# A sparse-expert tail on one Trainium2 core: the first work list reversed, the last tile's rows in a place of their own, and the hand-over between the layers dealt anew

## The chip, the cores and the metric

One core of a Trainium2 chip runs the whole program. The metric is the device time of one execution in microseconds (us). TensorE (PE) multiplies and transposes, VectorE (DVE), ScalarE (ACT) and GpSimd (POOL) compute, SyncE (SP) only issues transfers; POOL issues the indirect ones. Each engine runs its own program in order and waits on semaphores.

## The reference, cut to what matters

```python
x = x + gnn(layernorm(x))                      # 3125 nodes, 256 wide, 50000 edges, two layers
logits = layernorm(x) @ router_w.T             # 8 experts
rw, re = top_k(softmax(logits), 2)             # each node picks two
for e in range(8):
    y = gelu(tokens @ w1[e] + b1[e]) @ w2[e] + b2[e]
    out = out + combine[:, e:e + 1] * y
```

## The kernel before, in words

The nodes lie in NT = 25 tiles of 128 rows; the last has 53. The first graph layer comes first. Then, until 446.33 us, a loop over the tiles t does the second and routes its rows: TensorE sums neighbours into PSUM; VectorE adds, takes the variance (`x2_and_var`), POOL the power (`root`), VectorE normalizes into a buffer `tok[t % KEPT]` (KEPT = 8) and stores the residual (`norm_and_sum`); TensorE turns the rows (`turn_token`) and scores them against the router (`score`). Every batch of 3 or 4 tiles is routed: `choose_experts` and `shares` (which needs ScalarE's Exp, `powers`), a prefix sum on TensorE (`prefix`), `place`, which gives each of a tile's two choices a row in a buffer `xs_dram` sorted by expert, and POOL's `scatter`, two indirect transfers for a tile.

A sorted expert's rows are worked in units of 256 rows (two halves of 128). For unit i SP loads the rows (`next_rows`), VectorE copies the expert's first weights (`keep_w1`) and the rows' node numbers and shares (`keep_meta`); TensorE transposes (`turn_rows`, L1635), multiplies into the hidden layer (`hidden`, L1644) and into the output (`result`, L1655); ScalarE copies the transposes (L1853), does the Gelu (L1859) and weighs the result (`weigh`, L1868); VectorE adds the bias (L1317); POOL adds each half into `out` by an indirect transfer that accumulates (`add_half`, L700 for the first 16 halves, L702 in the loop). I number the units from 0 and the halves from 0, so unit i has the halves 2i and 2i+1. The same node can stand in halves of two experts, so a half may have to wait until earlier halves have landed: `before_it`, read from the table `tab_wi`, says how many.

Experts are ranked by their counts in the first three batches. The first EARLY = 8 units are listed from the full units of the first four batches (`list_first`), so that they can begin while the last batch is still being routed. The rest of the list is made from all counts (`list_rest`) and starts again with rank 0. When the row counts are final (semaphore `ends`, in `place` of the last batch), SP writes 256 rows of padding behind each expert's last row (`pad_experts`, L431, eight transfers of 264 KB); unit 8's rows may be loaded only when all eight have landed (the wait at L575) and all scatters too.

The order of all this on each engine is written out by hand. Before the change VectorE runs, after the last tile: units 2 and 3 (weights, meta), `reached_by_batch` (L1263 to L1270), result 0, `choose_experts`, unit 4, result 1, `shares`, `place`, unit 5, result 2, `list_rest`, unit 6, result 3, `tables`, unit 7, result 4.

Of the kernel before, what the change touches and what calls it, by code (L numbers as in the profile page):

```python
# [5 lines left out]
F32 = mybir.dt.float32  # L6
# [3 lines left out]
ALU = mybir.AluOpType  # L10
# [4 lines left out]
P = 128  # L15
# [4 lines left out]
def build(nc, x, src, dst, w1l, w1r, b1, w2l, w2r, b2, router_w, ew1, eb1, ew2, eb2, out):  # L20
# [64 lines left out]
    with ExitStack() as ctx:  # L85
# [169 lines left out]
        at_row = later([1], F32)  # L255
        at_rest = later([1], F32)
# [32 lines left out]
        step_first = summed_first[:, NE - 3, :]  # L289
# [55 lines left out]
        rest = expert([NE], F32)  # L345
        tab_ef = expert([NTAB], F32)
# [89 lines left out]
        def _(sp):  # L436
# [160 lines left out]
        def _(pool):  # L597
# [59 lines left out]
            def scatter(t, j):  # L657

                pool.wait_ge(S["slots"], j + 1)
                pool.sem_inc(S["pool_held"], 1)  # L660
                for k in range(TOPK):
                    g.indirect_dma_start(xs_dram, bass.IndirectOffsetOnAxis(  # L662
                        ap=slots[:, t * TOPK + k:t * TOPK + k + 1], axis=0),
                        tok[t % KEPT], None).then_inc(scattered[t % 2], 16)
# [95 lines left out]
        def _(dve):  # L760
# [344 lines left out]
            def norm_and_sum(t):  # L1105

                k, alone = t % KEPT, t == 0
                dve.wait_ge(S["tok_free"], t + 1)
                dve.wait_ge(S["rstd_in"], t + 1)
                v.tensor_scalar(tok[k][:, 0:D], zt[:, :], stat[:, 6:7], stat[:, 8:9], ALU.subtract, ALU.mult  # L1110
                                ).then_inc(S["normed"], 1)
# [3 lines left out]
                v.tensor_tensor(uo, zt[:, :], tok[k][:, 0:D], ALU.add).then_inc(S["u_ready"], 1)  # L1115
# [49 lines left out]
            def place(j):  # L1165

                dve.wait_ge(S["prefix"], j + 1)
                of = prefix_of(j)
                link(v.tensor_tensor(pos, of[:, 0:BATCH * NE].rearrange("p (t e) -> p t e", e=NE),
                                     hist[:, j:j + 1, :].to_broadcast((P, BATCH, NE)), ALU.add))  # L1170
                last = v.tensor_tensor(hist[:, j + 1, :], hist[:, j, :], of[:, BATCH * NE:(BATCH + 1) * NE], ALU.add)
                if j == NB - 1:
                    link(last)
                    v.tensor_copy(end_i, hist[:, NB, :]).then_inc(S["ends"], 1)
                for k in range(TOPK):
                    last = v.tensor_tensor(posm.rearrange("p (t k) e -> p t k e", k=TOPK)[:, :, k, :],
                                           mask.rearrange("p (t k) e -> p t k e", k=TOPK)[:, :, k, :], pos, ALU.mult)
                link(last)
                for q in range(IN_BATCH[j]):
                    t = FIRST_OF[j] + q  # L1180
                    v.tensor_copy(tok[t % KEPT][:, D:XW], meta[:, t:t + 1, :].rearrange("p t c -> p (t c)"))
# [12 lines left out]
            def order_experts():  # L1194
# [15 lines left out]
                v.memset(id_step[:, NE - 1:NE], float(NE))  # L1210
                link(v.scalar_tensor_tensor(at_row, iota_e[:, 0:1], REGION / PAIR, at_p, ALU.mult, ALU.add))
# [11 lines left out]
            def list_first():  # L1223
# [5 lines left out]
                v.tensor_copy(first[:, 0:1], cum_first[:, 0:1])  # L1229
                link(v.tensor_tensor(first[:, 1:NE], cum_first[:, 1:NE], cum_first[:, 0:NE - 1], ALU.subtract))  # L1230
                v.tensor_scalar(first_h, first, 2.0, None, ALU.mult)
                v.tensor_scalar(skip_rest, id_step, REGION / PAIR, None, ALU.mult)
                link(v.scalar_tensor_tensor(step_first, id_step, REGION / PAIR, first, ALU.mult, ALU.subtract))
                v.scalar_tensor_tensor(at_rest, first[:, 0:1], float(-EARLY), at_row, ALU.add, ALU.add)
                v.tensor_tensor(skip_rest[:, 0:NE - 1], skip_rest[:, 0:NE - 1], first[:, 1:NE], ALU.add)
# [3 lines left out]
                v.scalar_tensor_tensor(bound_first, each_expert(cum_first[:, 0:NE - 1], n - 1), 2.0, got[:, 0:n - 1, 1:NE],  # L1239
                                       ALU.mult, ALU.add)  # L1240
                link(v.tensor_tensor(weight_first, up_first[:, 1:, 0:NE - 1], up_first[:, 0:n - 1, 0:NE - 1], ALU.subtract))
                v.tensor_scalar(entry_first[:, 0:1], entry_first[:, 0:1], at_row, 4.0, ALU.add, ALU.mult)
                v.tensor_scalar(entry_first[:, 1:2], entry_first[:, 1:2], iota_e[:, 0:1], None, ALU.add)
                link(v.scalar_tensor_tensor(terms_w, bound_first.rearrange("p b e -> p (b e)"), at_p,
# [8 lines left out]
            def tables(of, n, lo, hi, halves_too):  # L1253
# [4 lines left out]
                v.tensor_scalar(tab_wi[:, 2 * lo:2 * hi], of[:, 2 * n + 2 * lo:2 * n + 2 * hi], float(halves_too), None, ALU.add  # L1258
                                ).then_inc(S["table"], 1)

            def reached_by_batch():
# [8 lines left out]
                v.tensor_tensor(weight[:, 0:NB - 1, :], reached[:, NB + 1:, 0:NE - 1], reached[:, NB:2 * NB - 1, 0:NE - 1],  # L1270
                                ALU.subtract)
# [53 lines left out]
            def early_unit(i):  # L1325

                dve.wait_ge(S["hid"], i - 1)
                keep_w1(i, i % 2)
                keep_meta(i, i % 2, 16 * (i // 2 + 1))
# [4 lines left out]
            for t in range(NT):  # L1334
# [6 lines left out]
                if t == LIST_AT:  # L1341
                    dve.wait_ge(S["listed"], 1)
                    tables(bank[2], EARLY, 0, EARLY, 0)
# [28 lines left out]
            dve.wait_ge(S["listed"], 2)  # L1372
            tables(bank[0], NTAB, EARLY, NTAB, 2 * EARLY)
# [14 lines left out]
        def _(pe):  # L1388
# [178 lines left out]
            def turn_token(t):  # L1567
                pe.wait_ge(S["normed"], t + 1 + NT)
                pe.wait_ge(S["nrm_t_in"], t + 2 * NT)
                for c in range(KD):  # L1570
                    last = te.transpose(bank[0][:, c * P:(c + 1) * P], tok[t % KEPT][:, c * P:(c + 1) * P], ident[:, :])  # L1571
                last.then_inc(S["nrm_tr"], 1)
# [75 lines left out]
            def result(i, s):  # L1648
                e = pe.value_load(tab_ei[0:1, bass.ds(i, 1)], min_val=0, max_val=NE - 1)
# [22 lines left out]
            def early_round(i):  # L1672

                result(i, i % 2)
# [7 lines left out]
            for i in range(4):  # L1682
                early_round(i)
            list_units(spread, bank[0], 2)
            for i in range(4, EARLY):
                early_round(i)
# [10 lines left out]
        def _(act):  # L1697
# [223 lines left out]
```

## Time and profile before

| | |
|---|---|
| median of 3 runs | 585.8 us (585.45 to 586.36) |
| the profiled execution, its own time | 586.81 us |
| its span in the trace | 584.8 us |
| busy: PE, DVE, ACT, POOL | 94%, 63%, 39%, 32% |
| granted TensorE clock, mean | 0.99 |

The span is that of one profiled execution and lies 2.0 us under its own time and 1.0 us under the median. Times in the trace are us from the start of the span.

### The profile page before, as it was taken

The numbers are of one execution on the slowest core, as the hardware profiler recorded it, in microseconds if no ns is written. First come the engines' busy times: TensorE is split into PE (matmuls) and PEld (weight loads), VectorE is DVE, ScalarE is ACT, GpSimd is POOL, SyncE is SP. The second block draws the span as 40 slices with busy tenths as digits, with TensorE's granted clock in tenths as the row PEclk, the third lists the DMA queues.
The fourth block names the chain that finished last, engine by engine and source line by source line (L and its number), as shares of the span: only waits on it lengthen the run. The fifth ranks groups of instructions, "written<-read, shape, count | busy, mean of one in ns | idle before, by whom it ended". The sixth has DMA issues, their size and how long they took to land.

```text
span 584.8 us, 11275 instructions
## 1 busy us (share of the span) xinstructions
PE 551.6 (94%) x3023; PEld 332.0 (57%) x3024; DVE 367.7 (63%) x1256; ACT 225.2 (39%) x427; POOL 185.1 (32%) x180
## 2 busy tenths in 40 slices
PE   5899999999999999999999999999998878999992
PEld 3445555555555555555445555555555767888881
DVE  6898677667676766765345667667877753444441
ACT  4666944444443444543100100000004544555652
POOL 4661000000000000000031034443446687587886
PEclk9999999999999999999999999999999989999997
DMA  8431121011011110111562135764335498668774
GB/s 255 143 91 55 55 63 55 29 55 54 28 55 42 41 55 28 55 49 33 119 208 82 55 118 181 239 214 137 127 102 179 120 253 139 122 127 130 124 127 47
DMA packets 64347, 61.29 MB, mean 105 GB/s; under 512 B 11281, under 2 KB 62334, under 8 KB 64302
## 3 DMA queue, kind: packets, MB, share of 16 engines
q1 hardware_dynamic: 48510, 45.92, 26.0%
q0 software_dynamic: 11200, 14.40, 13.0%
q10 hardware_dynamic: 4592, 0.41, 0.6%
q8 instruction: 23, 0.38, 0.3%
q14 instruction: 22, 0.18, 0.1%
HBM read 32.34 MB, written 29.30 MB: 105 GB/s over the span
## 4 chain that ended last, share of the span: by engine, by line
PE 71%; issue 9%; DMA 8%; DVE 5%; POOL 3%; POOLq 2%; ACT 0%; DVEq 0%; SPq 0%; ACTq 0%
PE bank L1497 22%; PE counts_ps L1497 13%; PE bank L1412 8%; PE bank L1487 7%; PE counts_ps L746 7%; PE bank L1655 5%; PE counts_ps L1644 5%; DMA out<-adj 3%; POOL xs_dram L662 2%; DMA y<-y_dram 2%; PE counts_ps L1635 1%; POOLq L690 1%; DMA xs_dram<-w,onehots 1%; PE bank L1402 1%; PE bank L1480 1%
## 5 line engine op out<-in xcount | busy, mean ns | idle before, releaser
L1497 PE MATMUL bank<-y,adj 128*128 128x512 f16 x625 | 154.7, 379 | 0.4 <-ACT zt L1731 0.4
L1497 PE MATMUL counts_ps<-y,adj 128*128 128x512 f16 x625 | 144.2, 379 | 1.9 <-DMA y<-y_dram 1.9
L753 ACT ACTIVATE adj<-counts_ps 128x1000 f32 (+1 forms) x80 | 80.2, 1004 | 59.0 <-PE counts_ps L746 59.0
L1497 PEld LDWEIGHTS counts_ps<-y,adj 128*128 128x128 f16 x625 | 60.5, 101 | 64.5 <-DMA y<-y_dram 4.2
L1497 PEld LDWEIGHTS bank<-y,adj 128*128 128x128 f16 x625 | 57.9, 97 | 59.5 <-issue 13.7
L639 POOL IOTA onehots<- 128x8 int32 x1 | 0.1, 143 | 225.7 <-PE counts_ps L746 225.7
L702 POOL DMA_INDIRECT out<-adj x40 | 62.9, 1572 | 18.2 <-issue 8.8
L1644 PE MATMUL counts_ps<-adj 128*128 128x256 f32 x240 | 56.9, 381 | 0.4 <-ACT adj L1853 0.4
L1655 PE MATMUL bank<-adj 128*128 x224 | 54.9, 389 | 2.4 <-issue 2.4
L746 PEld LDWEIGHTS counts_ps<-onehots 125*128 125x128 f16 x640 | 42.5, 98 | 23.9 <-ACT adj L753 11.2
L732 DVE TENSOR_TENSOR onehots<-iota,lo_t 125x1024 f16<-125x1024 f16 x80 | 54.9, 686 | 1.7 <-issue 0.9
L732 DVE TENSOR_TENSOR onehots<-iota,key_t 125x1000 f16<-125x1000 f16 x80 | 53.8, 673 | 0.0
L1830 ACT ACTIVATE rows<-bank 128x256 f32<-128x256 f32 x25 | 9.6, 382 | 113.3 <-PE bank L1571 113.3
L746 PE MATMUL counts_ps<-onehots 125*128 125x125 f16 x640 | 51.0, 221 | 0.5 <-DVE onehots L732 0.5
L1412 PE MATMUL bank<-w,rows 128*128 128x512 f32 x100 | 48.2, 604 | 3.0 <-issue 1.6
L1644 PEld LDWEIGHTS counts_ps<-adj 128*128 128x128 f32 x240 | 45.2, 190 | 7.1 <-ACT adj L1848 0.6
L1487 PE MATMUL bank<-w,rows 128*128 128x512 f32 x100 | 47.0, 592 | 0.0
L1655 PEld LDWEIGHTS bank<-adj 128*128 128x128 f32 x224 | 41.4, 195 | 8.0 <-issue 3.3
L1868 ACT ACTIVATE adj<-adj 128x256 f32<-128x256 f32 x56 | 25.4, 503 | 41.2 <-DVE adj L1317 41.2
L655 POOL TENSOR_TENSOR stat<-stat 128x1 f32<-128x1 f32 x25 | 14.2, 567 | 73.8 <-DVE stat L1103 73.8
L1724 ACT ACTIVATE yo<-bank,scl_i 128x256 f16<-128x256 f32 x23 | 10.9, 473 | 58.7 <-PE bank L1487 58.7
L1317 DVE TENSOR_TENSOR adj<-bank,adj 128x512 f32<-128x512 f32 x28 | 19.4, 692 | 20.7 <-PE bank L1655 18.8
(283 smaller groups left out, 670.9 us busy)
## 6 DMA issues: line engine op xcount, KB each, us to landing
adj<-xs_dram SPq DMA_DIRECT2D x31, 264.0 KB, 3.2
rows<-z_dram SPq DMA_DIRECT2D x49, 128.0 KB
z_dram<-zt SPq DMA_DIRECT2D x33, 128.0 KB, 1.7
adj<-in_L_ffn_w SPq DMA_DIRECT2D x16, 256.0 KB, 3.2
rows<-in_x SPq DMA_DIRECT2D x24, 128.0 KB
out<-yo SPq DMA_DIRECT2D x24, 128.0 KB
y_dram<-yo SPq DMA_DIRECT2D x23, 128.0 KB, 1.7
y<-y_dram SPq DMA_DIRECT2D x4, 640.0 KB, 6.8
```

Of the source, the lines that this page charges most:

```text
L655: g.tensor_tensor(stat[:, 8:9], stat[:, 9:10], stat[:, 10:11], ALU.pow).then_inc(S["rstd_in"], 1)
L702: g.indirect_dma_start(out, at, ye[u][:, h, :], None, bounds_check=N - 1, oob_is_err=False, compute_op=ALU.add).then_inc(landed[q % NLAND] ...
L732: last = nc.vector.tensor_tensor(oh[0:RUN, slot, :].rearrange("p (g k w) -> p g k w", k=n, w=HALF), iota_4[0:RUN, 0:n, :].rearrange("p (g ...
L746: last = nc.tensor.matmul(counts_ps[:, 2 * slot + bank_of, at * P:at * P + KEYS], stat_g[:, :, h:h + 1].rearrange("p k a -> p (k a)"), mov ...
L753: nc.scalar.activation(adj[:, :, bass.ds(at, GW * WD)].rearrange("p b (h d) -> p b h d", d=WD), counts_ps[:, 2 * (group % 2):2 * (group % ...
L1317: v.tensor_tensor(ysum[s], y_ps[s], ew(eb2_sb, e, 0).rearrange("p (h n) -> p h n", h=1) .to_broadcast((P, 2, D)), ALU.add).then_inc(S["ysu ...
L1412: last = te.matmul(out_of[t % 2][:, :], nrm_t_of[t % 2][:, k * P:(k + 1) * P], w[:, k, :], start=(k == 0), stop=(k == KD - 1))
L1487: last = te.matmul(bank[1][:, :], nrm_t[:, k * P:(k + 1) * P], w[:, k, :], start=(k == 0), stop=(k == KD - 1))
L1497: last = te.matmul(to, adj[:, b, t * P:(t + 1) * P], y[:, b, :], start=(b == 0), stop=(b == NT - 1))
L1644: last = te.matmul(hid_ps[s][:, m * PAIR:(m + 1) * PAIR], w1_of[s][:, k, m * P:(m + 1) * P], xe_t[s][:, k * PAIR:(k + 1) * PAIR], start=(k ...
L1655: last = te.matmul(y_ps[s][:, h, :], ge_t[s][:, m * PAIR + h * P:m * PAIR + (h + 1) * P], ew(ew2_sb, e, m), start=(m == 0), stop=(m == KD ...
L1868: a.activation(ye[u][:, h, :], ysum[s][:, h, :], ACT.Copy, scale=tab_c[:, bass.ds(i * 2 + h, 1)]).then_inc(S["ye_in"], 1)
```

## The change

- **First list reversed.** The first 8 units come in the reverse order of the ranks, so that the last of them and unit 8 are of the same expert (rank 0). `list_first` finds a position p by `at_rev` = 7 - p and `at_less` = p - 16 instead of `at_p`; the number added to `before_it` in the rest of the list is no longer 16 but 16 less the halves of rank 0 in the first list (`list_base`), and those are added back for every later expert (one more instruction in `reached_by_batch`).
- **Own place for the last tile's rows.** Tile 24 is normalized into `tok_last` and no longer into the buffer of tile 16. POOL therefore doesn't wait, after the scatter of tile 17, until that of tile 16 has landed.
- **The tail's order.** On VectorE result 0 comes straight after unit 3; `shares` follows `choose_experts`; unit 4 is split, its weights before result 1 and its meta after `place`; `reached_by_batch` comes after result 2, and `list_rest` after unit 6. ScalarE does the last Exp before the transposes of unit 3 and the Gelu of unit 2, and the dummy Gelu is gone. SP loads unit 6 before it writes the first three paddings, and writes five after unit 7 where it wrote two. TensorE reads the expert number of a unit (`expert_of`) one unit ahead in the first 8 units, and multiplies out the rest of the list (`list_units`) after result 4 and not before it.

```diff
@@ SP
-            row = row_of(6)
+            next_rows(6, row_of(6))
+            row = row_of(7)
             pad_experts(sp, range(0, 3))
-            next_rows(6, row)
-            row = row_of(7)
-            pad_experts(sp, range(3, 6))
             next_rows(7, row)
-            pad_experts(sp, range(6, NE))
+            pad_experts(sp, range(3, NE))
@@ POOL, scatter
-                if 0 < t <= NT - KEPT:
+                if 0 < t < NT - KEPT:
                     pool.wait_ge(scattered[(t - 1) % 2], ((t - 1) // 2 + 1) * (16 * TOPK))
                     pool.sem_inc(S["tok_free"], 1)
@@ DVE, list_first
-                v.scalar_tensor_tensor(terms_2, cum_first, at_p, id_step, ALU.is_le, ALU.mult, accum_out=entry_first[:, 1:2])
-                v.scalar_tensor_tensor(terms_1, cum_first, at_p, step_first, ALU.is_le, ALU.mult, accum_out=entry_first[:, 0:1])
+                v.scalar_tensor_tensor(terms_2, cum_first, at_rev, id_step, ALU.is_le, ALU.mult, accum_out=entry_first[:, 1:2])
+                v.scalar_tensor_tensor(terms_1, cum_first, at_rev, skip_rest, ALU.is_le, ALU.mult, accum_out=entry_first[:, 0:1])
+                v.tensor_scalar(list_base, first_h[:, 0:1], -1.0, float(2 * EARLY), ALU.mult, ALU.add)
@@ DVE, reached_by_batch
+                v.tensor_tensor(weight[:, 0, 0:1], weight[:, 0, 0:1], first_h[:, 0:1], ALU.add)
@@ DVE, after the last tile
             early_unit(2)
             early_unit(3)
-            reached_by_batch()
             early_result(0)
             choose_experts(NB - 1)
-            early_unit(4)
+            shares(NB - 1)
+            early_weights(4)
             early_result(1)
-            shares(NB - 1)
             place(NB - 1)
+            early_meta(4)
             early_unit(5)
             early_result(2)
+            reached_by_batch()
+            early_unit(6)
             list_rest()
-            early_unit(6)
             early_result(3)
             dve.wait_ge(S["listed"], 2)
-            tables(bank[0], NTAB, EARLY, NTAB, 2 * EARLY)
+            tables(bank[0], NTAB, EARLY, NTAB, list_base)
@@ PE
+            e = expert_of(0)
+            for i in range(EARLY):
+                result_of(e, i, i % 2)
+                if i + 1 < EARLY:
+                    e = expert_of(i + 1)
...
+                if i == 4:
+                    list_units(spread, bank[0], 2)
                 hidden(i + 2, i % 2)
                 turn_rows((i + 3) % 2, 16 * ((i + 3) // 2 + 1))
@@ ACT
                 if i == 0:
                     weigh(0, 0, 0)
+                    powers(NB - 1)
+                    turn_rows(3, 1)
                 gelu(i + 2, i % 2)
-                turn_rows(i + 3, (i + 3) % 2)
-                if i == 0:
-                    powers(NB - 1)
-                    a.activation(scl[:, 14:15], scl[:, 8:9], ACT.Gelu)
-                else:
+                if i > 0:
+                    turn_rows(i + 3, (i + 3) % 2)
                     weigh(i, i // UNITS, i % UNITS)
```

On VectorE, between unit 3's meta (L1302) and result 0 (L1314, L1317), the program before holds the seven instructions of `reached_by_batch`:

```order
L1302 SCALAR_TENSOR_TENSOR adj<-adj 128x2 x2
L1263 TENSOR_TENSOR adj<-onehots 128x56
L1265 TENSOR_SCALAR adj<-adj 128x56
L1266 TENSOR_SCALAR adj<-adj 128x112
L1267 CAST adj<-adj 128x112
L1268 TENSOR_TENSOR adj<-adj,onehots 128x112
L1269 TENSOR_SCALAR adj<-adj 128x112
L1270 TENSOR_TENSOR adj<-adj 128x42
L1309 TENSOR_LOAD adj
L1309 ISA x2
L1314 CAST adj<-adj 128x2
L1317 ISA
```

The changed program has at the same place on VectorE (its line numbers are some 8 higher; L1134 is the first instruction of `choose_experts`):

```order
L1310 SCALAR_TENSOR_TENSOR adj<-adj 128x2 x2
L1317 TENSOR_LOAD adj
L1317 ISA x2
L1322 CAST adj<-adj 128x2
L1325 ISA
L1325 TENSOR_TENSOR adj<-bank,adj 128x512
L1134 COPY onehots<-bank 128x32
```

So result 0 stands directly behind unit 3 there, and the seven are now behind result 2.

On SP, after the load of unit 5, the program before reads unit 6's row number (L522) and goes straight to the first padding (L430, L431), which waits for `ends`:

```order
L525 DMA adj<-xs_dram 128x2x264
L522 TENSOR_LOAD adj
L522 ISA x2
L430 TENSOR_LOAD onehots [waits zeros,ends]
L430 ISA x2
L431 ISA
L431 DMA xs_dram<-biases 128x2x264
```

The changed program issues unit 6's load (L532) first, which waits for `meta_in` and `xe_tr`, and only then the first padding (L437, L438):

```order
L529 TENSOR_LOAD adj
L529 ISA x2
L532 ISA [waits meta_in,xe_tr]
L532 DMA adj<-xs_dram 128x2x264
L529 TENSOR_LOAD adj
L529 ISA x2
L437 TENSOR_LOAD onehots [waits zeros,ends]
L437 ISA x2
L438 ISA
L438 DMA xs_dram<-biases 128x2x264
```

The load of unit 6 has moved from behind three paddings to ahead of all eight, and with it the paddings are now queued behind unit 4's meta.

On ScalarE, behind the weighing of unit 0 (L1888), the changed program has the Exp (L1854), unit 3's transposes (L1873) and then unit 2's Gelu (L1879), each function with its table load:

```order
L1888 ACTIVATE adj<-adj 128x256 [waits landed1]
L1854 ACT_TABLE_LOAD
L1854 ACTIVATE onehots<-onehots 128x32 [waits top]
L1873 ACTIVATE adj<-counts_ps 128x512 [waits xe_tr]
L1876 TENSOR_LOAD adj
L1876 ISA x2
L1879 ISA [waits hid]
L1879 ACT_TABLE_LOAD
```

Before, the Gelu and the transposes stood ahead of the Exp; the number of table loads is the same.

## Rows read from the trace of the kernel before

**Rows 1.** The page: the span
```profile
span 584.8 us, 11275 instructions
```

**Rows 2.** The chain in order of time: start, us, what; pieces of the tail
```profile
478.65 4.41 DMA out<-adj
483.26 3.34 DMA adj<-xs_dram
...
576.03 3.68 DMA out<-adj
...
580.78 1.55 POOL out L702
```

**Rows 3.** POOL's timeline: halves 10, 15, 16, 54; in brackets the idle time before
```profile
489.79 1.55 POOL L700 DMA_INDIRECT out<-adj  x1 [2.18 <-ACT adj L1868]
...
499.69 1.55 POOL L700 DMA_INDIRECT out<-adj  x1 [0.31 <-DMA out<-adj]
505.62 1.55 POOL L702 DMA_INDIRECT out<-adj  x1 [4.39 <-issue]
...
577.88 1.55 POOL L702 DMA_INDIRECT out<-adj  x1 [0.31 <-issue]
```

**Rows 4.** ScalarE's timeline: a table load; units 5, 8 and 27 weighed
```profile
461.31 1.28 ACT L1834 ACT_TABLE_LOAD   x1
...
488.48 0.91 ACT L1868 ACTIVATE adj<-adj 128x256 f32<-128x256 f32 x2 [0.54 <-DVE adj L1317]
...
498.49 0.91 ACT L1868 ACTIVATE adj<-adj 128x256 f32<-128x256 f32 x2 [1.07 <-DVE adj L1317]
...
572.57 0.91 ACT L1868 ACTIVATE adj<-adj 128x256 f32<-128x256 f32 x2 [1.41 <-DVE adj L1317]
```

**Rows 5.** TensorE's timeline: last tile, result 4, hidden 7, transposes 8, result 6
```profile
453.12 0.44 PE L1571 MATMUL bank<-ident,w 128*128 128x128 f32 x2 [1.05 <-DVE w L1110]
...
474.87 3.54 PE L1655 MATMUL bank<-adj 128*128 x8 [1.24 <-issue]
...
483.46 1.89 PE L1644 MATMUL counts_ps<-adj 128*128 128x256 f32 x8
486.65 0.66 PE L1635 MATMUL counts_ps<-ident,adj 128*128 128x128 f32 x4 [1.30 <-DMA adj<-xs_dram]
487.56 1.99 PE L1655 MATMUL bank<-adj 128*128 x8 [0.25 <-issue]
```

**Rows 6.** SP's queue in time: the last two paddings
```profile
477.25 1.50 SPq L431 DMA_DIRECT2D xs_dram<-biases  x2
```

**Rows 7.** SP's instructions of L575, 477.3 to 480: duration in ns, first and last start
```profile
L575 SPq EVENT_SEMAPHORE  x1: 3375/3375/3375, 479.5 to 479.5; - x1
```

**Rows 8.** POOL's timeline: the first scatter of tile 18
```profile
446.96 1.20 POOL L662 DMA_INDIRECT xs_dram<-w,onehots  x1 [2.74 <-DMA xs_dram<-w,onehots]
```

**Rows 9.** VectorE's timeline: last norm, reached, result 0, choose's end, ends, slots
```profile
452.65 0.41 DVE L1110 TENSOR_SCALAR w<-zt,stat 128x256 f32<-128x256 f32 x1 [1.99 <-POOL stat L655]
...
455.63 0.21 DVE L1263 TENSOR_TENSOR adj<-onehots 128x56 int32<-128x56 f32 x1
...
457.30 0.20 DVE L1270 TENSOR_TENSOR adj<-adj 128x42 f32<-128x42 f32 x1
...
458.45 0.69 DVE L1317 TENSOR_TENSOR adj<-bank,adj 128x512 f32<-128x512 f32 x1
...
461.75 0.16 DVE L1152 TENSOR_TENSOR onehots<-onehots 128x16 f16<-128x16 f16 x1
...
465.78 0.17 DVE L1174 CAST onehots<-onehots 128x8 int32<-128x8 f32 x1
...
466.83 0.17 DVE L1187 CAST onehots<-onehots 128x8 uint32<-128x8 f32 x1
```

**Rows 10.** Windows: us, PE busy, PEld, DVE, ACT, POOL, granted clock, DMA share, GB/s
```profile
472.00:474.00 2.00, 0.72 (x5) 0.52 (x5) 1.76 (x12) 1.20 (x3) 1.70 (x2) 1.00 0.80 298
...
476.00:477.00 1.00, 1.00 (x4) 0.82 (x3) 0.68 (x4) 0.79 (x2) 0.69 (x2) 0.50 1.06 267
```

More of the change, by code:

```diff
@@ L255, in build @@
         at_row = later([1], F32)
+        at_rev = later([1], F32)
+        at_less = later([1], F32)
+        list_base = later([1], F32)
         at_rest = later([1], F32)
@@ L345, in build, with tok_of @@
         rest = expert([NE], F32)
+        tok_last = expert([XW], F32)
+        def tok_of(t):
+            return tok[t % KEPT] if t < NT - 1 else tok_last
         tab_ef = expert([NTAB], F32)
@@ L1105, in norm_and_sum @@
             def norm_and_sum(t):
-                k, alone = t % KEPT, t == 0
-                dve.wait_ge(S["tok_free"], t + 1)
+                alone = t == 0
+                dve.wait_ge(S["tok_free"], min(t + 1, NT - 1))
                 dve.wait_ge(S["rstd_in"], t + 1)
-                v.tensor_scalar(tok[k][:, 0:D], zt[:, :], stat[:, 6:7], stat[:, 8:9], ALU.subtract, ALU.mult
+                v.tensor_scalar(tok_of(t)[:, 0:D], zt[:, :], stat[:, 6:7], stat[:, 8:9], ALU.subtract, ALU.mult
                                 ).then_inc(S["normed"], 1)
@@ L1180, in place @@
                     t = FIRST_OF[j] + q
-                    v.tensor_copy(tok[t % KEPT][:, D:XW], meta[:, t:t + 1, :].rearrange("p t c -> p (t c)"))
+                    v.tensor_copy(tok_of(t)[:, D:XW], meta[:, t:t + 1, :].rearrange("p t c -> p (t c)"))
                 link(v.tensor_reduce(slot_f, posm, AX.X, ALU.add))
@@ L1210, in order_experts @@
                 v.memset(id_step[:, NE - 1:NE], float(NE))
+                v.tensor_scalar(at_rev, at_p, -1.0, float(EARLY - 1), ALU.mult, ALU.add)
+                v.tensor_scalar(at_less, at_p, float(-2 * EARLY), None, ALU.add)
                 link(v.scalar_tensor_tensor(at_row, iota_e[:, 0:1], REGION / PAIR, at_p, ALU.mult, ALU.add))
@@ L1229, in list_first @@
                 v.tensor_copy(first[:, 0:1], cum_first[:, 0:1])
+                v.tensor_scalar(skip_rest, id_step, REGION / PAIR, None, ALU.mult)
                 link(v.tensor_tensor(first[:, 1:NE], cum_first[:, 1:NE], cum_first[:, 0:NE - 1], ALU.subtract))
                 v.tensor_scalar(first_h, first, 2.0, None, ALU.mult)
-                v.tensor_scalar(skip_rest, id_step, REGION / PAIR, None, ALU.mult)
-                link(v.scalar_tensor_tensor(step_first, id_step, REGION / PAIR, first, ALU.mult, ALU.subtract))
@@ L1234, in list_first @@
                 v.scalar_tensor_tensor(at_rest, first[:, 0:1], float(-EARLY), at_row, ALU.add, ALU.add)
-                v.tensor_tensor(skip_rest[:, 0:NE - 1], skip_rest[:, 0:NE - 1], first[:, 1:NE], ALU.add)
-                v.scalar_tensor_tensor(terms_2, cum_first, at_p, id_step, ALU.is_le, ALU.mult, accum_out=entry_first[:, 1:2])
-                v.scalar_tensor_tensor(terms_1, cum_first, at_p, step_first, ALU.is_le, ALU.mult, accum_out=entry_first[:, 0:1])
+                link(v.tensor_tensor(skip_rest[:, 0:NE - 1], skip_rest[:, 0:NE - 1], first[:, 1:NE], ALU.add))
@@ L1251, in list_first, with tables @@
                 last.then_inc(S["spread"], 1)
-            def tables(of, n, lo, hi, halves_too):
+            def tables(of, n, lo, hi, base):
                 v.tensor_scalar(tab_ri[:, lo:hi], of[:, lo:hi], float(PAIR // 4), float(NE * REGION), ALU.mult, ALU.min)
@@ L1325, in early_unit, with early_weights, early_meta @@
             def early_unit(i):
+                early_weights(i)
+                early_meta(i)
+            def early_weights(i):
                 dve.wait_ge(S["hid"], i - 1)
                 keep_w1(i, i % 2)
+            def early_meta(i):
                 keep_meta(i, i % 2, 16 * (i // 2 + 1))
@@ L1342, in _ @@
                     dve.wait_ge(S["listed"], 1)
-                    tables(bank[2], EARLY, 0, EARLY, 0)
+                    tables(bank[2], EARLY, 0, EARLY, 0.0)
                 norm_and_sum(t)
@@ L1570, in turn_token @@
                 for c in range(KD):
-                    last = te.transpose(bank[0][:, c * P:(c + 1) * P], tok[t % KEPT][:, c * P:(c + 1) * P], ident[:, :])
+                    last = te.transpose(bank[0][:, c * P:(c + 1) * P], tok_of(t)[:, c * P:(c + 1) * P], ident[:, :])
                 last.then_inc(S["nrm_tr"], 1)
@@ L1648, in result, with result_of @@
             def result(i, s):
-                e = pe.value_load(tab_ei[0:1, bass.ds(i, 1)], min_val=0, max_val=NE - 1)
+                result_of(pe.value_load(tab_ei[0:1, bass.ds(i, 1)], min_val=0, max_val=NE - 1), i, s)
+            def result_of(e, i, s):
                 pe.wait_ge(S["ge_in"], i + 1)
@@ L1670, in _, with expert_of @@
             pe.sem_inc(S["ysum_in"], 2)
-            def early_round(i):
-                result(i, i % 2)
+            def expert_of(i):
+                return pe.value_load(tab_ei[0:1, bass.ds(i, 1)], min_val=0, max_val=NE - 1)
+            e = expert_of(0)
[3 more added lines that the diff above has]
+                    e = expert_of(i + 1)
                 if i == 0:
@@ L1678, in early_round @@
                     prefix(NB - 1)
+                if i == 4:
+                    list_units(spread, bank[0], 2)
                 hidden(i + 2, i % 2)
                 turn_rows((i + 3) % 2, 16 * ((i + 3) // 2 + 1))
[L1682 to L1686, printed above, removed]
             pe.wait_ge(S["table"], 2)
```

19 lines of the change are left out of this document (9 added, 10 removed).

## The prediction

> **What bounds the kernel now.** Everything the change touches lies in the last quarter of the span [rows 1], so I started at the end of the chain of waits and read back. The last unit's second half (half 55) starts on POOL at 580.78, 1.07 us after the transfer of half 53, begun at 576.03, has landed (3.68 later, 579.71) [rows 2]. Before that POOL issues one half after another. From half 16 at 505.62 to half 54 at 577.88 are 38 steps in 72.26 us, 1.90 each [rows 3]. ScalarE has weighed what POOL issues long before: unit 8 is weighed from 498.49, its first half starts at 505.62, 7.13 later; for unit 27 it is 572.57 and 577.88, 5.31 later [rows 3, 4]. Where POOL really waits for ScalarE, the step is 1.31 (unit 5: 488.48 to 489.79 [rows 3, 4]). So from 505.62 on POOL sets the end, though the chain names TensorE for most of that stretch: it follows the semaphore that came last by its record. The date of half 16 is what has to be explained.
>
> Half 16 follows half 15 (499.69) by 5.93 us, an idle time of 4.39 that the trace calls issue [rows 3]. No engine's work ends it. But in the program before every half of the rest of the list asks for at least 16 landed halves, so half 16 needs the landing of half 15, issued just before it.
>
> Half 15 in turn hangs on unit 7, and that on TensorE's stream, which last stood still before unit 8's transposes at 486.65, waiting for that unit's rows [rows 5]. They were loaded at 483.26, and here the chain puts the wait down to a transfer of POOL's from 478.65 [rows 2], which is again only the last record. SP's own instructions show it: the wait at L575, for the eight paddings, lasts 3.375 us from 479.5 to 482.9 [rows 7]. The last padding was issued by 477.25 + 1.50 = 478.75 [rows 6] and so landed 4.1 later. SP had started on the paddings as soon as `ends` was set, at 465.78 + 0.17 = 465.95 on VectorE [rows 9], and worked through them and two loads without waiting for anybody.
>
> **The change, step by step.**
>
> *The last norm.* POOL idled 2.74 us before tile 18's scatter for the landing of tile 16's [rows 8]; VectorE then idled 1.99 for POOL's power and TensorE 1.05 for VectorE's norm [rows 5, 9]. With a place of its own for tile 24 the first is gone. POOL's power comes 2.35 earlier at most (two scatters are still ahead of it, and VectorE's variance), so VectorE gains its 1.99 and TensorE its 1.05.
>
> *Result 0.* `reached_by_batch` takes 455.63 to 457.50, 1.87 us, and no longer stands ahead of it. Result 0 goes from 458.45 to 458.45 - 1.99 - 1.87 = 454.6. TensorE's side: last turn at 453.12 - 1.05 = 452.1, 0.44 for it, some 2.1 for the result, 454.6 too.
>
> *From result 0 to `ends`.* Now 465.95 - 458.45 = 7.5 us, with choose, unit 4, result 1, shares and half of `place` in it [rows 9]. The same pieces are there afterwards in another order, but unit 4's meta (0.4) has gone behind `place`, whose rest takes 467.0 - 465.95 = 1.05. So meta 4 ends at 454.6 + 7.5 + 1.05 = 463.15. `shares` now waits early for the Exp: ScalarE weighs unit 0 from 455.3 for 0.91, loads the table in 1.28 [rows 4] and is done near 457.8; choose ends 461.91 - 458.45 = 3.46 after result 0 [rows 9], at 458.1. It fits with 0.3 to spare. Unit 2's Gelu, behind both table loads, ends near 460.5, half a us before TensorE wants it; should it be late, TensorE has slack (below). The Trainium skill (ScalarE: Activation LUTs, Table sets) puts a switch of tables at about 2.7 us. The trace has 1.28, and by that figure the Exp, hence everything to the end, would come 1.1 us later than I say.
>
> *SP.* Unit 6's load and all paddings now wait for meta 4 (463.15) where they waited for `ends` (465.95). Behind that SP does the same eight paddings, two loads and two reads of row numbers as before, only in another order. So the last padding is issued 2.8 us earlier, near 476.0, and unit 8's rows are loaded at 480.5 instead of 483.26, if the landing still takes 4.1. The bounds: 0, if the transfers themselves are the limit; and at most as much as TensorE could use, next.
>
> *TensorE.* It reads the expert number ahead, which saves the 0.25 before result 6 [rows 5]. After `list_units` (VectorE: meta 4 at 463.15, then unit 5, result 2, the seven moved instructions, unit 6 and `list_rest`, together 9.7 us, so 472.9 as now) it has hidden 6, transposes 7, result 5 and hidden 7 left, 5.9 us: done at 479. Now hidden 7 ends at 483.46 + 1.89 = 485.35. So without the rows of unit 8 being late TensorE would gain 6; with them at 480.5 + 3.34 = 483.85 it gains 2.8 + 0.25 = 3.05 and stands idle for nearly 5 us, where it now stands for 1.30.
>
> *The clock.* That idle time has a price. Between 471.7 and 474.87 TensorE did almost nothing (0.72 busy in 472 to 474), and then ran at 0.50 of its clock, 1.2 GHz and not 2.4 [rows 10]: result 4 took 3.54 us, against 1.99 for result 6, 1.55 lost [rows 5]. Now this loss is hidden, because it falls ahead of the wait for unit 8. Afterwards the long pause comes last, and the slow stretch lies on result 6 and hidden 8, in the open. I charge 1.55 once. Left for TensorE: 1.5. Bounds 3.05 (no fall) and about 0 (a longer slow stretch).
>
> *Half 16.* The added number becomes 16 less the halves of rank 0 in the first list. Counting the router's choices for the reference's inputs, ranks 0, 1, 2 get 3, 3, 2 of the 8 units; so half 16 asks for 10, all long landed. What is left of the 5.93 is between one plain step, 1.90, and one issue plus the 1.07 that POOL needs from the end of a wait to its next transfer, 1.55 + 1.07 = 2.62 [rows 2, 3]. Nothing says that its loop is entered without cost, so I take 2.62: 3.3 us saved, 4.0 at most. Within the first list, reversed, halves 4 and 5 ask for the halves three places back instead of five and six, 5.6 us back at 1.86 a step, more than the landings of 3.7 to 4.4 [rows 2]. No new wait.
>
> *Other edits.* The few added instructions of `order_experts` and `list_first` lie under TensorE's sums of a tile; uncovered they would be some 0.2 us each. POOL reaches half 2 some 4 us earlier, since `slots` does (467.0 to 462.7 [rows 9]); halves 2 to 15 then fill 26 us and aren't the limit at a gain under 6.
>
> *Sum.* Half 15 starts 1.5 earlier, half 16 1.5 + 3.3 = 4.8. Does POOL still set the end? Its lag behind ScalarE at unit 8 falls from 7.13 to 3.8, and by the 1.8 that it makes up over the loop to 2.0 at unit 27, over the 1.31 of a real wait. It does, barely. So the span goes from 584.8 to 580.0, and the median, 1.0 above the span [rows 1], from 585.8 to **581.0**.
>
> **The rivals.**
> - *No fall of the clock.* TensorE's pause is split by other work, as now at 485.35, where 1.3 idle left the clock alone. Then 3.05 + 3.3 = 6.35: 579.5. Against it: the pause I expect is longer than the one before 474.87.
> - *The paddings land no sooner.* The DMA share is 0.80 at 472 to 474 and 1.06 at 476 to 477 [rows 10]; if bytes and not issues are the limit, unit 8's rows come when they do now, and only 0.25 + 3.3 less the clock's 1.55 is left, 2.0: 583.8. The Trainium skill (DMA: Bandwidth & Descriptors, Issuing engines are not separate DMA queues) says that transfers of all issuing engines interleave on the same 16 engines; POOL's adds begin earlier here and so run into the paddings. For the gain speaks that before 470 these engines were half idle, and the paddings move there.
> - *Unit 8's rows are not late.* If the padding goes out much faster ahead of POOL's adds, TensorE gets near its 6: 6 + 3.3 gives 576.7 at best.
> - *The list change doesn't do it.* If the 4.39 at half 16 is the entry into POOL's loop and no landing, 1.5 remains: 584.3. Against it: ScalarE enters its own loop with 1.07 idle [rows 4].
> - *Slower.* One mechanism could do it, the clock. At 0.50 each us costs half a us. If TensorE, once slow after a pause of 5 us, stayed so, the 6.35 would be eaten after 12.7 us of it, and each unit more would cost 3.9 us. Up to now one slow stretch ended by itself before result 5.
>
> **How the numbers follow.** Chances: as forecast 0.45, no fall of the clock 0.24, paddings no sooner 0.12, unit 8 not late 0.06, list change without effect 0.07, slower 0.03, the rest spread. A measurement here tells 0.2% (1.2 us) from no change. Faster by more: all but about half of the list case, and the slower one: 0.88; within 0.2%: 0.09; slower: 0.03. The range takes in the forecast with its bounds (clock, 4.0 for half 16) and the first two rivals: 577.6 to 584.3.
>
> **What would show it.** VectorE's last norm without its 1.99 idle; result 0 near 454.6; slots at 462.7; SP's wait for the paddings still there, ending near 480.1; TensorE idle for 4 us or more before unit 8's transposes near 483.9; a stretch at 0.50 right behind it; and half 16 at most 2.7 us after half 15, near 501. I would be wrong if the gap of half 16 stayed above 4, if the paddings took over 5 us to land, or if POOL in the loop showed waits for ScalarE.

## The result and the profile after

The changed kernel takes 582.55 us (median of 5 runs, 580.24 to 583.07) against 586.24 for the kernel before beside it: ratio 0.9933, interval 0.9915 to 0.9952. Two more sets on other chips, `after_again` and `after_third`, gave 0.9930 each. (One execution of the kernel before, beside `after_again`, took 1163.3 us and is left out of the ratios.) The forecast of 581.0 had the sign, and its range the time; it was 1.55 too low. Of these, 0.44 is the kernel before itself, which took 586.24 beside it and not 585.8: the gain was 3.7 where 4.8 was forecast.

The profiled execution took 583.07 with a span of 581.2, where [rows 1] has 584.8, and where the tail begins it runs 0.44 earlier than that of before. That much is chance: the traces of `after_again` and `after_third` reach this place 1.3 and 1.4 later than this one. TensorE's timeline (start, us, in brackets the idle time before), lines 1652 transposes, 1674 results, 1661 hidden layers:

```profile
451.48 0.38 PE L1588 MATMUL bank<-ident,adj 128*128 128x128 f32 x2
...
476.33 1.89 PE L1661 MATMUL counts_ps<-adj 128*128 128x256 f32 x8
482.92 1.12 PE L1652 MATMUL counts_ps<-ident,adj 128*128 128x128 f32 x4 [4.70 <-DMA adj<-xs_dram]
483.83 3.62 PE L1674 MATMUL bank<-adj 128*128 x8
487.24 1.98 PE L1661 MATMUL counts_ps<-adj 128*128 128x256 f32 x8
489.06 0.60 PE L1652 MATMUL counts_ps<-ident,adj 128*128 128x128 f32 x4
```

The rows of [rows 5] are all there, earlier, but the pause before unit 8's transposes has grown from 1.30 to 4.70 and result 6 takes 3.62 instead of 1.99. The windows (stretch, its length, busy time of PE, PEld, DVE, ACT and POOL, then the granted clock, the DMA share and GB/s) show the clock falling behind the pause:

```profile
477.00:480.00 3.00, 1.22 (x6) 0.74 (x4) 0.00 (x0) 1.10 (x3) 2.39 (x3) 1.00 0.95 163
480.00:484.00 4.00, 1.08 (x5) 1.08 (x6) 0.63 (x7) 0.00 (x0) 2.35 (x2) 0.57 0.97 198
484.00:487.00 3.00, 3.00 (x9) 2.37 (x8) 1.61 (x8) 1.51 (x3) 0.98 (x1) 0.50 0.60 130
```

SP's queue; the last of the four paddings is issued by 470.81 + 4.87 = 475.68, and unit 8's rows are asked for at 479.22:

```profile
470.81 4.87 SPq L438 DMA_DIRECT2D xs_dram<-biases  x4
479.22 1.76 SPq L532 DMA_DIRECT2D adj<-xs_dram  x2
```

Between them stands SP's instruction of L580, the wait for the eight paddings (ns, least, median, most; the long one is 2,512 from 476.3 on, so to 478.8, where [rows 7] has 3,375):

```profile
L580 SPq EVENT_SEMAPHORE  x2: 28/1270/2512, 476.3 to 478.9; - x2
```

VectorE: last norm, result 0, `ends`, `slots`. The 1.99 of idle time of [rows 9] is gone:

```profile
450.00 0.41 DVE L1115 TENSOR_SCALAR adj<-zt,stat 128x256 f32<-128x256 f32 x1
...
453.82 0.69 DVE L1325 TENSOR_TENSOR adj<-bank,adj 128x512 f32<-128x512 f32 x1 [0.24 <-PE bank L1674]
...
460.72 0.17 DVE L1179 CAST onehots<-onehots 128x8 int32<-128x8 f32 x1
...
461.87 0.19 DVE L1192 CAST onehots<-onehots 128x8 uint32<-128x8 f32 x1
```

ScalarE: units 3, 8 and 27 are weighed. Ahead of unit 3 it stands idle for 4.41:

```profile
473.47 0.91 ACT L1888 ACTIVATE adj<-adj 128x256 f32<-128x256 f32 x2 [4.41 <-DVE adj L1325]
...
496.43 0.91 ACT L1888 ACTIVATE adj<-adj 128x256 f32<-128x256 f32 x2 [1.06 <-DMA out<-adj]
...
570.68 0.91 ACT L1888 ACTIVATE adj<-adj 128x256 f32<-128x256 f32 x2 [1.60 <-DVE adj L1325]
```

POOL: a scatter that no longer waits, then halves 15, 16, 17, 38, 39, 54, 55:

```profile
444.10 0.96 POOL L667 DMA_INDIRECT xs_dram<-w,onehots  x1 [0.30 <-issue]
...
497.63 1.55 POOL L705 DMA_INDIRECT out<-adj  x1 [0.30 <-DMA out<-adj]
500.18 1.55 POOL L707 DMA_INDIRECT out<-adj  x1 [1.00 <-DMA out<-adj]
502.30 1.55 POOL L707 DMA_INDIRECT out<-adj  x1 [0.57 <-DMA out<-adj]
...
543.43 1.73 POOL L707 DMA_INDIRECT out<-adj  x1 [0.31 <-issue]
545.47 1.55 POOL L707 DMA_INDIRECT out<-adj  x1 [0.30 <-issue]
...
574.21 1.55 POOL L707 DMA_INDIRECT out<-adj  x1 [0.30 <-issue]
577.14 1.55 POOL L707 DMA_INDIRECT out<-adj  x1 [1.38 <-issue]
```

Against [rows 3], half 15 starts 2.06 earlier and half 16 5.44 earlier. But half 54 starts only 3.67 earlier. Between them lie 74.03 us for 38 steps, where before there were 72.26: 1.77 of the gain is given back inside the loop. POOL's lag behind ScalarE (start of a unit's first half less start of its weighing) goes from 3.75 at unit 8 to 3.53 at unit 27, where I had it fall to 2.0. This is what the experiments had to explain first.

One row above gives a hint: half 38's transfer is 1.73 long, not 1.55. From unit 8 on 12 transfers of the even halves last over 1.6 us, up to 1.79, and the start after a long one comes later. VectorE at that place:

```profile
542.46 0.69 DVE L1325 TENSOR_TENSOR adj<-bank,adj 128x512 f32<-128x512 f32 x1 [0.76 <-PE bank L1674]
543.32 0.43 DVE L1330 COPY adj<-adj 128x512 f32 x1 [0.17 <-issue]
```

The copy of the weights starts at 543.32, 0.11 ahead of POOL's 543.43. At each of the long ones it starts 0.05 to 0.19 ahead, and in the kernel before at five of its six (units 15 and 20 to 23, at a lag near 6; the sixth is in unit 11, where the copy starts 1.14 behind POOL). A unit takes POOL 3.71 where it is free, and the copies come every 3.89 as TensorE does. So my theory was: POOL gains on ScalarE until its start falls just behind a copy's, and then each unit's gain is taken back; one such lag is near 6.0, another near 4.0, and the changed kernel starts its loop at 3.75.

### The profile page after: what moved, and what is told of

Same layout as the page of the kernel before. It is cut to its first block, busy times and chain, and to the rows that moved or that the text cites. A ratio compares the mean times of both kernels' runs of the same rounds, so it can differ in the third digit from the quotient of the medians.

```text
span 581.2 us, 11275 instructions
## 1 busy us (share of the span) xinstructions
PE 551.5 (95%) x3023; PEld 332.8 (57%) x3024; DVE 366.5 (63%) x1259; ACT 225.1 (39%) x426; POOL 184.7 (32%) x180
## 4 chain that ended last, share of the span: by engine, by line
PE 64%; issue 11%; DMA 11%; POOL 5%; DVE 4%; POOLq 4%; ACT 0%; SPq 0%; DVEq 0%; ACTq 0%
PE bank L1514 23%; PE counts_ps L1514 13%; DMA out<-adj 8%; PE bank L1429 8%; PE counts_ps L751 7%; PE bank L1504 7%; POOLq L695 2%; POOL xs_dram L667 2%; DMA y<-y_dram 2%; PE bank L1419 1%; POOLq L700 1%; PE bank L1674 1%; PE bank L1497 1%; POOL out L707 1%; PE bank L1599 1%
## 5 line engine op out<-in xcount | busy, mean ns | idle before, releaser
L707 POOL DMA_INDIRECT out<-adj x40 | 64.2, 1604 | 15.3 <-issue 7.5
L1429 PE MATMUL bank<-w,rows 128*128 128x512 f32 x100 | 49.4, 617 | 2.1 <-issue 2.0
L1504 PE MATMUL bank<-w,rows 128*128 128x512 f32 x100 | 47.0, 592 | 0.0
L1888 ACT ACTIVATE adj<-adj 128x256 f32<-128x256 f32 x56 | 25.4, 503 | 38.8 <-DVE adj L1325 32.3
```

Of the source, the lines that this page charges most:

```text
L707: g.indirect_dma_start(out, at, ye[u][:, h, :], None, bounds_check=N - 1, oob_is_err=False, compute_op=ALU.add).then_inc(landed[q % NLAND] ...
L1429: last = te.matmul(out_of[t % 2][:, :], nrm_t_of[t % 2][:, k * P:(k + 1) * P], w[:, k, :], start=(k == 0), stop=(k == KD - 1))
L1504: last = te.matmul(bank[1][:, :], nrm_t[:, k * P:(k + 1) * P], w[:, k, :], start=(k == 0), stop=(k == KD - 1))
L1888: a.activation(ye[u][:, h, :], ysum[s][:, h, :], ACT.Copy, scale=tab_c[:, bass.ds(i * 2 + h, 1)]).then_inc(S["ye_in"], 1)
```

## The experiments

**The list alone** (`list_alone`). The kernel before with the edits of the change that belong to the list, and nothing else (cut):

```diff
-                v.scalar_tensor_tensor(terms_2, cum_first, at_p, id_step, ALU.is_le, ALU.mult, accum_out=entry_first[:, 1:2])
+                v.scalar_tensor_tensor(terms_2, cum_first, at_rev, id_step, ALU.is_le, ALU.mult, accum_out=entry_first[:, 1:2])
...
-            tables(bank[0], NTAB, EARLY, NTAB, 2 * EARLY)
+            tables(bank[0], NTAB, EARLY, NTAB, list_base)
```

> The kernel before with the reversed first list and nothing else of the change. If the 5.93 us between halves 15 and 16 were the wait for a landing, the gap becomes 2.6 and half 16 starts 3.3 earlier, near 502.3. If the pause is the entry into POOL's loop, the gap stays 5.9 and the time stays 585.8. What reaches the end depends on the second theory, the one on POOL's slow transfers: POOL's lag behind ScalarE would be 3.8 at unit 8, and if a copy on VectorE holds POOL at a lag of about 4 it is still about 3.5 at unit 27 (before 5.3): 1.8 us gained, 584.0. If nothing holds it there, POOL goes on at 1.86 a half until it waits for ScalarE at a lag of 1.3 to 2: all 3.3 gained, 582.5.

Ratio 0.9974 (0.9953 to 0.9995): 1.5 us faster. POOL at half 16:

```profile
497.15 1.55 POOL L703 DMA_INDIRECT out<-adj  x1 [0.30 <-DMA out<-adj]
500.04 1.66 POOL L705 DMA_INDIRECT out<-adj  x1 [1.34 <-DMA out<-adj]
```

The gap is 2.89. The lag at unit 8 is 4.09, 13 transfers are long, and it is still 3.48 at unit 27. The wait for a landing is shown, and so is that less than the 3.3 reaches the end: the interval allows 2.7 at most. Beside it, TensorE's pauses of 1.93 and 0.98 brought no fall of the clock (1.00 from 478 to 490).

**The change without its list** (`list_undone`), the same edits taken out of the changed kernel.

> The changed kernel with the first list in rising order of ranks again. Landing theory: the gap before half 16 goes from 2.55 back to 5.9, half 16 near 503.5, lag behind ScalarE 7.1 at unit 8. With the hold at a lag of 4 in the changed kernel, this one catches up as the kernel before did, to 5.3 at unit 27, and loses only about 1.8: 584.4. Without such a hold it loses 3.3: 585.9. If the list does nothing: 582.5.

Ratio 0.9983 (0.9966 to 1.0000); half 16 5.73 after half 15, lag 6.93 and then 5.88. Since the changed kernel hadn't run on this chip, I ran it again beside it (`list_undone_2`):

> The first list in rising order of ranks again, beside the changed kernel. Half 16 comes 5.7 us after half 15 and not 2.6, which puts POOL's lag behind ScalarE at 7 instead of 4 at unit 8. At a lag of 7 no copy of VectorE meets POOL's transfers, so this kernel catches up by about 1 to 1.2 us over the loop and the changed one by none: 2.0 us slower than the changed kernel (range 1.2 to 3.1). Rival, no hold: 3.1 slower.

583.90 (0.9979, 0.9961 to 0.9997) against 581.31 for the changed kernel (`after_third`): the list is worth 2.6, between the two theories. By the spread of the two sets it can be 0.9 more or less, so this doesn't tell 2.0 from 3.1. Half 16 with its old wait:

```profile
501.12 1.55 POOL L708 DMA_INDIRECT out<-adj  x1 [3.94 <-issue]
```

**Tile 24 in tile 16's place** (`tok_undone`).

```diff
-            return tok[t % KEPT] if t < NT - 1 else tok_last
+            return tok[t % KEPT]
...
-                if 0 < t < NT - KEPT:
+                if 0 < t <= NT - KEPT:
...
-                dve.wait_ge(S["tok_free"], min(t + 1, NT - 1))
+                dve.wait_ge(S["tok_free"], t + 1)
```

> The changed kernel with tile 24's rows again in the place of tile 16's. Theory that this wait was on the path: POOL waits 2.7 us before tile 18's scatter again, VectorE's last norm comes some 2 us later (452.3 for 450.0), result 0 at 455.8, and with it slots, paddings and unit 8's rows; unit 8's transposes 2 us later and the end too: 584.5. Rival: Exp, tables and paddings have enough slack of their own, so result 0 moves and unit 8's rows do not: within 0.5 of 582.5.

The median was 583.62 (0.9980, 0.9958 to 1.0001), yet in the profiled execution unit 8's transposes came no later than in the changed kernel. The two didn't agree, so again beside the changed kernel (`tok_undone_2`):

> Tile 24's rows in the place of tile 16's again, now beside the changed kernel. In the first run's trace result 0 came 1.75 us later (455.57 for the weighing of unit 0, half 2 at 469.05 for 468.05), yet unit 8's transposes came as in the changed kernel, since the landing of the paddings takes up the difference. Theory from that: no difference on the path, within 1 us of the changed kernel. Rival, from the first run's median (0.9980 of before, where the changed kernel has 0.993): about 2.5 us slower than the changed kernel.

582.97 (0.9967, 0.9948 to 0.9987) against 581.31: 1.7 slower. The two sets together, each against the kernel before beside it, put this kernel 2.4 behind the changed one (by my estimate from their spread 1.4 to 3.3), so my theory of no difference is wrong. POOL in this execution:

```profile
446.40 0.96 POOL L667 DMA_INDIRECT xs_dram<-w,onehots  x1 [2.26 <-DMA xs_dram<-w,onehots]
```

And TensorE, unit 8's transposes:

```profile
485.28 1.11 PE L1652 MATMUL counts_ps<-ident,adj 128*128 128x128 f32 x4 [4.78 <-DMA adj<-xs_dram]
```

The wait is back, unit 0 is weighed at 456.82 instead of 455.92 in the changed kernel beside it, and unit 8's transposes start at 485.28 instead of 483.68. A single pair of traces can't price the wait: in the three traces of the changed kernel itself unit 0 is weighed at 454.54, 455.80 and 455.92, and the last padding lands 2.9 to 3.9 behind its issue in the traces of these kernels.

**The copy in another mode** (`reduce_copy`; the edit is cut, and holds from unit 8 on).

```diff
-                v.tensor_copy(w1_of[s].rearrange("p k n -> p (k n)"),
-                              ew1_sb[:, bass.ds(e, 1), :].rearrange("p a n -> p (a n)")).then_inc(S["w1_in"], 1)
...
+                    last = v.tensor_reduce(to, of.rearrange("p (n b) -> p n b", b=1), AX.X, ALU.add)
```

> The changed kernel, where VectorE moves the weights of units 8 to 27 with a sum over an axis of one element instead of the copy: the same bytes, another mode of the engine (about 0.6 to 0.7 us instead of 0.43). Theory: POOL's transfers take 1.66 to 1.79 us instead of 1.55 in the even halves of units 9 to 14 and 18 to 24 because the fast copy starts with them and keeps POOL out. Then all of them take 1.55, POOL's step falls from 3.89 to 3.71 a unit, its lag behind ScalarE falls from 3.5 to between 1.3 and 2 at unit 27, and the time to 580.5 to 581.0. The Trainium skill (SBUF - State Buffer, Who interferes with whom) says that a copy in the two-port mode and a GpSimd instruction shut each other out and that tensor_reduce never contends. Rival: the longer transfers are POOL's own or the DMA engines' (the same halves stay long), time 582.5; or the longer VectorE instruction delays TensorE and it is slower.

POOL's transfers from half 16 on (ns, least, median, most), first in the changed kernel, then here:

```profile
L707 POOL DMA_INDIRECT out<-adj x40: 1547/1549/1794, 500.2 to 577.1; - x40
```

```profile
L707 POOL DMA_INDIRECT out<-adj x40: 1547/1549/1566, 500.3 to 576.2; - x40
```

Not one is long, although VectorE's instruction now lasts 0.69. It isn't that the two no longer meet: here too some begin 0.10 to 0.19 behind VectorE's instruction, as half 42:

```profile
551.20 0.69 DVE L1334 TENSOR_REDUCE adj<-adj 128x512 f32 x1 [0.16 <-issue]
551.30 1.55 POOL L707 DMA_INDIRECT out<-adj  x1 [0.30 <-issue]
```

So it is the form of the copy, not its bytes and not the timing. By the Trainium skill (SBUF — State Buffer, Who interferes with whom) a copy in a two-port mode and an instruction of GpSimd exclude each other, and whichever begins first shuts the other out for the whole of its length. The trace agrees that the copy holds up the transfer and the reduction doesn't, but not on the rest. The price is at most 0.24 of the copy's 0.43, and a copy that begins at 568.70 in the kernel before, 0.09 behind a transfer of POOL's, takes its 0.43. What the 40 transfers take over 1.55 each sums to 2.2 us in the changed kernel's first trace, and to nothing here. The time, however, was 581.69 (0.9941, 0.9920 to 0.9961), no better than the changed kernel's ratio, and the lag at unit 27 was 2.81, not under 2. Two things stand behind that. POOL has other short waits here, 0.55 to 0.65 before halves 24 to 27, put down to landings; and the hold is not always there: in the three traces of the changed kernel 12, 8 and 3 transfers are long, and in the third the lag does fall, from 3.77 to 2.16 in 72.36 us. From half 16 to 54 the 2.2 us of the long transfers are gone in `reduce_copy`, but POOL's other waits have grown by 1.4, and these steps take 73.27 us, only 0.76 less than 74.03. So it is shown that the copy lengthens the transfers; that this alone costs the end of the kernel anything is not. In `list_undone` only one transfer is long, and the lag still falls by no more than 1.05.

**Three paddings on ScalarE** (`split_pads`), and the changed kernel beside it (`after_again`, 581.50).

```diff
-            pad_experts(sp, range(3, NE))
+            pad_experts(sp, range(3, SP_PADS))
...
+                    if i == 3:
+                        pad_experts(act, range(SP_PADS, NE))
                     weigh(i, i // UNITS, i % UNITS)
```

(`SP_PADS` is 5.)

> The changed kernel, where ScalarE issues the last three of the eight paddings ahead of the third unit's weighing, at about 469 to 473, where it stands idle for 4.41 us. Theory: what holds unit 8's rows is SP's issuing (last padding at 475.3) and a landing of some 3 us behind it. Then SP has issued its last near 471 and ScalarE near 473, the wait ends near 476, unit 8's rows are asked for near 476.5 instead of 479.2 and TensorE's transposes start near 480 instead of 482.9, with a pause under 2 us and no fall of the clock (result 6 in 2.0 instead of 3.6): 2.9 + 1.6, so about 4 us less than the changed kernel beside it. Rival: the bytes on the DMA engines are the limit (paddings and adds together), the wait ends when it does now, near 478.8, and the time is the changed kernel's.

577.84 (0.9877, 0.9854 to 0.9901), 3.7 less than the changed kernel (1.5 to 5.2 by the spread of the two sets). ScalarE's issues lie in its idle time:

```profile
468.49 3.57 ACTq L440 DMA_DIRECT2D xs_dram<-biases  x3
473.17 0.91 ACT L1890 ACTIVATE adj<-adj 128x256 f32<-128x256 f32 x2 [5.09 <-DVE adj L1327]
```

TensorE waits 0.68 for unit 8's rows, where the changed kernel waits 4.70 in its first trace and 2.38 in that of `after_again`, and result 6 takes 1.89:

```profile
479.68 0.67 PE L1654 MATMUL counts_ps<-ident,adj 128*128 128x128 f32 x4 [0.68 <-DMA adj<-xs_dram]
480.18 1.89 PE L1676 MATMUL bank<-adj 128*128 x8
```

In `after_again` the two were:

```profile
483.54 0.66 PE L1652 MATMUL counts_ps<-ident,adj 128*128 128x128 f32 x4 [2.38 <-DMA adj<-xs_dram]
484.04 3.22 PE L1674 MATMUL bank<-adj 128*128 x8
```

SP's wait for the paddings ends at 476.1 instead of 478.8 in the changed kernel's first trace, so the rival, that bytes set the time, is out. The same edit in the kernel before (`before_split`):

> The kernel before, where ScalarE issues the last three paddings ahead of unit 3's weighing and nothing else is changed. Theory: paddings are worth only what TensorE can use, and here it has its own work until 485.35 and waits 1.30 us for unit 8's rows; half 16 waits for the landing of half 15 as before. So at most 1.3 us faster, and perhaps nothing, since ScalarE weighs unit 3 up to 1.5 us later: 0.997 to 1.001 of the kernel before. Rival: the paddings are the bound on their own, whatever the order of the rest, and it gains the 3 to 4 us that they gave in the changed kernel.

0.9990 (0.9972 to 1.0008): nothing that stands out of the noise, and 1.6 us at most. There SP's wait ended at 481.2 (before 482.9) and half 16 waited as ever, so the paddings are worth their 3.7 only behind the rest of the change.

**Filling TensorE's pause** (`filled`).

```diff
                 hidden(i + 2, i % 2)
+                if i == 5:
+                    for _ in range(38):
+                        te.transpose(bank[1][:, 0:P], ident[:, :], ident[:, :])
                 turn_rows((i + 3) % 2, 16 * ((i + 3) // 2 + 1))
```

> The changed kernel with 38 idle transposes (128x128, 0.11 us each, about 4.1 us) on TensorE behind hidden 7, which nobody reads. Theory: the pause of 4.7 us before unit 8's transposes drops the clock to 0.50, and result 6 costs 3.6 instead of 2.0. With the filling the clock stays at 1.0, result 6 takes 2.0, results 6 and 7 come 1.6 earlier and the end 1.6 earlier than that of the changed kernel beside it. Rival: the slow stretch has its cause further ahead (the 2.5 us without work before list_units at 472), the clock falls all the same and the time is the changed kernel's, or up to 0.5 more if the filling reaches past the rows' arrival.

579.36 (0.9894, 0.9879 to 0.9908), 2.1 less than the changed kernel (0.2 to 3.4 by the spread of the two sets). TensorE's timeline, L1708 being the filling:

```profile
480.51 4.31 PE L1708 MATMUL bank<-ident 128*128 128x128 f32 x38
484.66 0.60 PE L1652 MATMUL counts_ps<-ident,adj 128*128 128x128 f32 x4
485.09 1.89 PE L1674 MATMUL bank<-adj 128*128 x8
```

From 478 to 490 the clock stays at 1.00 and result 6 takes 1.89, although TensorE does nothing useful in these 4.31 us. The rival is out: here too the clock fell further ahead (0.57 from 474 to 476, after the 2.49 without work before `list_units`), and it had come back before result 6. The filling reaches about 1 us past the rows' arrival, so that unit 27 is weighed only 0.6 earlier than in `after_again`'s trace. The rest of that pair's difference is POOL's lag at unit 27 (2.28 for 4.02), which the filling doesn't touch. So it is shown that the filling holds the clock; of the 2.1, the traces put no more than 0.6 down to it.

**Both** (`split_reduce`).

> Both: three paddings on ScalarE, and VectorE's move of the weights from unit 8 on as a sum over one element. If both theories hold the time is the changed kernel's less 4 (paddings) and less 0.7 (the reduced hold, as far as the run alone showed: lag 2.8 instead of 3.5 at unit 27). If POOL becomes the bound once TensorE is 4.5 earlier, the second part is worth more, up to 2 us, since POOL then runs at 1.85 a half without the steps of 2.05.

575.91 (0.9835, 0.9812 to 0.9859): 9.6 us faster than before, and the best kernel here. Over `split_pads` it gains 1.9, more than the copy's mode gave alone, but by the spread of the two sets it can be anything from nothing to 3.8. Its lag fell only from 3.97 to 3.07, against 3.92 to 3.21 in `split_pads`, so it isn't shown that this gain comes from the hold.

The tail's new order was never undone by itself. Undoing the list costs 2.6 and undoing tile 24's own place costs 1.7. Together that is already more than the 3.7 of the change, so the parts don't simply add up, and what the order is worth stays open.

## Why the prediction was right, and where it failed

- **Last norm, result 0.** Predicted 454.6, measured 453.82, or 454.26 with the 0.44 of this execution; in the other two traces of the changed kernel unit 0 is weighed 1.3 later than here. The wait is gone; it is worth 1.7 at the end (`tok_undone_2`).
- **From result 0 to `slots`.** Predicted 462.7, measured 461.87 + 0.19. The Exp came in time, with tables loaded in 1.28 each.
- **SP.** The last padding was issued at 475.7 (predicted 476.0). The landing term was mis-sized: 3.1 behind it and not 4.1, so unit 8's rows were asked for at 479.22 and not 480.5. That the transfers themselves are not the limit, `split_pads` shows.
- **TensorE and its clock.** A pause of nearly 5 was predicted, 4.70 came, and the slow stretch behind it. Charged were 1.55; result 6 alone lost 1.63, the transposes 0.5 more. This and the earlier rows about cancel, which is luck: half 15 starts 2.06, 1.94 and 2.08 earlier in the three traces, against 1.5 in the sum. `filled` shows that with work in the pause result 6 isn't slow.
- **Half 16.** Predicted 2.62 behind half 15, measured 2.55, and 2.57 in the other two traces. Shown both ways, by `list_alone` and `list_undone_2`.
- **The step that failed** is in the sum: "by the 1.8 that it makes up over the loop to 2.0 at unit 27". I took the rate of catching up from the kernel before, as if it belonged to POOL alone. In the profiled execution it made up 0.2: from half 16 to 54 it needed 74.03 us and not 72.26. Of these 1.77 us, 1.31 are longer transfers, which come from where POOL's starts lie against VectorE's copies, and 0.46 short waits. Half 16 had come 5.44 earlier where the sum has 4.8, so the last halves come 1.1 later than in the sum, as the gain of 3.7 falls short of 4.8 by 1.1. In the other two traces of the changed kernel POOL lost 0.3 (that execution took 583.32) and made up 1.6 (581.38). What sets the rate as a whole stays open, since without any long transfer it was 0.96 in `reduce_copy`.
- **Rivals.** Paddings that land no sooner, a list without effect, rows that aren't late and a clock that stays up: none occurred. Two side sums were off. TensorE's gain without late rows was counted from the end of hidden 7, 485.35, and not from the transposes' start, 486.65: it is 7.65 and not 6, and that rival's time near 575. And the bounds given (3.05 and 4.0) reach down to 578.7; the 577.6 of the range is worked out nowhere.

## What to carry to other kernels

When a wait is removed ahead of two engines of nearly equal pace (here 3.71 and 3.89 a unit), don't extrapolate the rate of catching up from the old lag: look for what the two meet at the new one. After such a change look at the engine that now idles longest. Here ScalarE's 4.41 us of idle time could carry three of SP's transfers, which gave as much again as the whole change, and next to nothing without it. And a pause that grows on TensorE can have a second price behind it, in slow matmuls.

## What the runs showed of the hardware

- A 128x512 fp32 copy on VectorE, 0.43 long, that starts 0.05 to 0.3 us ahead of an indirect DMA on POOL lengthens it, and the more the closer they are: the transfer ends 1.84 after the copy's start (0.07 ahead: 1.77; 0.11: 1.73; 0.20: 1.65; 0.26: 1.59; from 0.30 on it keeps its 1.55). So it goes in seven traces, with one exception at 0.05 in `after_third`. The same move as a reduction, 0.69 long, doesn't lengthen it. A few transfers are long with a copy that starts 1.14 to 1.22 behind them (1.65 to 1.73).
- Pauses of TensorE of 1.93 and 0.98 left the granted clock at 1.00, one of 4.70 was followed by 0.50 (1.2 instead of 2.4 GHz). Over all the traces, pauses of up to 1.98 before unit 8's transposes left result 6 at 1.89 to 1.99, and those of 2.38 to 4.78 were followed by one of 2.75 to 3.62, though not the longest by the slowest (4.10: 2.88; 2.38: 3.22). Nor is the pause's length all: after 2.50 without work before `list_units` hidden 6 took 1.97 in the changed kernel's first trace, and after 2.51 in `after_again` 3.20.
- Before half 32 POOL stands idle longer in every trace (1.16 in the changed kernel's, 0.95 to 1.81 in all). A new round of its loop begins there, but so it does at halves 24, 40 and 48, where it waits 0.6 at most. Why is open; no run looked for it.
